# Moving two row sums from ScalarE to VectorE and four elementwise steps from VectorE to GpSimd in the last stage of a transformer layer

## The reference

```python
def quantize_e4m3(t, scale):
    return jnp.clip(t / scale, -FP8_MAX, FP8_MAX).astype(_FP8_DTYPE)
...
scores = jnp.einsum('bhqd,bhkd->bhqk', q, k) / np.sqrt(HD)
attn = jax.nn.softmax(scores.astype(jnp.float32), axis=-1)
out = jnp.einsum('bhqk,bhkd->bhqd', attn, v)
...
x_mat = quantize_e4m3(x2d, SCALE).astype(jnp.float16)
w_mat = quantize_e4m3(weight, SCALE).astype(jnp.float16)
out2d = (x_mat @ w_mat.T).astype(jnp.float32) * (SCALE * SCALE)
out2d = out2d + bias
...
x = _layernorm(x + _L0_attn_ref(...), axis=-1)
x = _layernorm(x + _L0_ffn_ref(x, L0_ffn_weight, L0_ffn_bias), axis=-1)
```

## Time and profile before

| | us |
|---|---|
| median of 2 timed runs | 1343.76 (1337.73 to 1349.79) |
| profiled execution | 1351.19 |
| its span on the slowest core (core 2) | 1349.6 |
| spans of the 8 cores | 1334.7 to 1349.6 |

### The profile page before, as it was taken

How to read it: one execution, slowest core, us unless ns; L and a number is a source line. 1 busy time by engine, 2 the same in 40 slices (tenths; PEclk the granted TensorE clock), 3 DMA queues, 4 the chain that set the end, 5 groups by cost and what they waited for, 6 DMA issues and landing times.

```text
span 1349.6 us, 11600 instructions; the slowest of 8 cores (1334.7 to 1349.6 us)
## 1 busy us (share of the span) xinstructions
PE 828.8 (61%) x3584; PEld 288.8 (21%) x3584; DVE 501.8 (37%) x942; ACT 724.7 (54%) x793; POOL 127.6 (9%) x66
## 2 busy tenths in 40 slices
PE   0588768595000587878878777877877723433334
PEld 0333323242000122222222222222222201111111
DVE  4267758621334112111211211121121165555566
ACT  0000000000221788888888888888888785555554
POOL 0046647500000000000000000000000000000000
PEclk9787767687555799999899999999999956666777
DMA  9732251203600000000000000000000000000001
GB/s 146 115 53 49 40 117 32 62 0 88 207 31 31 16 1 0 1 1 1 1 1 1 1 0 1 0 1 1 0 1 0 1 16 16 31 32 32 32 32 78
DMA packets 15131, 42.79 MB, mean 32 GB/s; under 512 B 2144, under 2 KB 2272, under 8 KB 15072
## 3 DMA queue, kind: packets, MB, share of 16 engines
q0 software_dynamic: 6624, 15.73, 6.7%
q1 hardware_dynamic: 8448, 26.33, 6.6%
HBM read 36.81 MB, written 8.39 MB: 33 GB/s over the span
## 4 chain that ended last, share of the span: by engine, by line
PE 31%; ACT 28%; DVE 14%; DMA 9%; issue 8%; POOL 7%; SPq 2%; ACTq 0%; DVEq 0%; POOLq 0%
ACT PT L397 18%; PE ps L412 14%; PE ps_sc L384 9%; PE ps L283 5%; DMA wfs<-wfT 3%; DMA srep_s<-srep 3%; POOL rs L248 2%; POOL rs L246 2%; POOL ro L249 2%; PE ps L219 1%; DVE zf L658 1%; SPq L261 1%; DMA wb<-wqT 1%; DVE zf L663 1%; DMA qT<-ro 1%
## 5 line engine op out<-in xcount | busy, mean ns | idle before, releaser
L397 ACT ACTIVATE PT<-ps_sc,k_s 128x1024 bf16<-128x1024 f32 x512 | 544.5, 1110 | 85.3 <-PE ps L412 47.4
L384 PE MATMUL ps_sc<-qT,kT 64*128 64x512 bf16 x1024 | 199.1, 388 | 228.3 <-ACT PT L397 215.6
L412 PE MATMUL ps<-PT,va 128*65 128x512 bf16 x1024 | 324.0, 399 | 24.5 <-ACT PT L397 24.2
L318 ACT ACT_TABLE_LOAD x1 | 1.3, 1283 | 336.2 <-DMA wfs<-wfT 336.2
L651 PE MATMUL ps<-wfq,yqT 128*128 128x512 bf16 x256 | 90.2, 531 | 141.0 <-ACT yqT L641 141.0
L219 PE MATMUL ps<-xT,wb 128*128 128x512 bf16 x512 | 147.2, 463 | 37.0 <-DVE qraw L230 30.2
L427 DVE COPY oa_sb<-ps 65x1024 f32<-65x1024 f32 x32 | 39.1, 1221 | 345.0 <-PE ps L412 345.0
L384 PEld LDWEIGHTS ps_sc<-qT,kT 64*128 64x128 bf16 x1024 | 58.5, 93 | 438.8 <-issue 436.6
L412 PEld LDWEIGHTS ps<-PT,va 128*65 128x65 bf16 x1024 | 72.6, 110 | 158.4 <-issue 158.4
L219 PEld LDWEIGHTS ps<-xT,wb 128*128 128x128 bf16 x512 | 57.9, 114 | 125.9 <-issue 125.9
L446 DVE RECIPROCAL rc_sb<-ps 128x1 f32<-128x1 f32 x256 | 20.1, 150 | 171.1 <-PE ps L434 171.0
(11 more groups left out here) (76 smaller groups left out, 581.1 us busy)
## 6 DMA issues: line engine op xcount, KB each, us to landing
xf<-x SPq DMA_DIRECT2D x1, 8192.0 KB, 33.2
out<-xf SPq DMA_DIRECT2D x16, 512.0 KB, 2.6
xb<-x POOLq DMA_DIRECT2D x1, 4096.0 KB, 33.4
qT<-ro SPq DMA_DIRECT2D x32, 128.0 KB, 2.4
kT<-ro SPq DMA_DIRECT2D x32, 128.0 KB, 2.4
wfs<-wfT POOLq DMA_DIRECT2D x8, 512.0 KB, 3.7
wb<-wqT POOLq DMA_DIRECT2D x1, 2048.0 KB, 17.9
wb<-wkT POOLq DMA_DIRECT2D x1, 2048.0 KB, 16.4
```

The source lines that it names most:

```text
L384: return e.matmul(ps_sc[:, slot, half * 512:(half + 1) * 512], kT[r0:r0 + 64, hp, kt * 128:(kt + 1) * 128], qT[r0:r0 + 64, hp, q0:q0 + 512 ...
L397: return e.activation(PT[:, slot, :], ps_sc[:, slot, :], AF.Exp, bias=consts[:, C_SHIFT:C_SHIFT + 1], scale=0.125)
L412: return e.matmul(ps1[0:65, base:base + 512], va[:, kt, h * 65: h * 65 + 65], PT[:, slot, half * 512:(half + 1) * 512], start=(kt == 0), s ...
```

## The change

`sum` and `sum2` become `reduce_sum` on DVE, and the ACT instructions that accumulated them go; `sq` and `sq2` stay on ACT and take over the waits. `qM`, `qE`, `qMt` and `z2` are the same instructions issued on POOL ("GC") instead of DVE. Everything else stands in the same order.

```diff
--- before.py
+++ after.py
@@ -547,16 +547,14 @@
         c0 = (st % 4) * 4
         c2_ = 16 + par * 4
         if stg == 0:
-            deps = [attn_done, t_wfq, rot_use["st1"].get(st % 4),
-                    rot_use["dump"][0]]
-            tk["sum"] = A("S", lambda e: e.activation(wfs[:], xf[:, st, :], AF.Copy,
-                                                      bias=0.0, scale=1.0,
-                                                      accum_out=stat[:, c0:c0 + 1]),
+            deps = [attn_done, t_wfq, rot_use["st1"].get(st % 4)]
+            tk["sum"] = A("V", lambda e: e.reduce_sum(stat[:, c0:c0 + 1], xf[:, st, :],
+                                                      axis=mybir.AxisListType.X),
                           waits=deps)
             tk["sq"] = A("S", lambda e: e.activation(wfs[:], xf[:, st, :], AF.Square,
                                                      bias=0.0, scale=1.0,
                                                      accum_out=stat[:, c0 + 1:c0 + 2]),
-                         waits=[tk["sum"]])
+                         waits=deps + [rot_use["dump"][0]])
             rot_use["dump"][0] = tk["sq"]
         elif stg == 1:
             tk["mean"] = A("V", lambda e: e.tensor_scalar_mul(stat[:, c0 + 2:c0 + 3],
@@ -595,13 +593,13 @@
                                                      scale=1.0), waits=[tk["qA"]])
         elif stg == 3:
             qs = qs_t if par == 0 else qs2
-            tk["qM"] = A("V", lambda e: e.tensor_scalar(qs[:, 0, :], qs[:, 1, :],
-                                                        consts[:, C_ILN2:C_ILN2 + 1],
-                                                        63.5, ALU.mult, ALU.add),
+            tk["qM"] = A("GC", lambda e: e.tensor_scalar(qs[:, 0, :], qs[:, 1, :],
+                                                         consts[:, C_ILN2:C_ILN2 + 1],
+                                                         63.5, ALU.mult, ALU.add),
                          waits=[tk["qL"], t_k])
-            tk["qE"] = A("V", lambda e: e.tensor_scalar(qs[:, 1, :], qs[:, 0, :],
-                                                        cder[:, 0:1], cder[:, 1:2],
-                                                        ALU.add, ALU.subtract),
+            tk["qE"] = A("GC", lambda e: e.tensor_scalar(qs[:, 1, :], qs[:, 0, :],
+                                                         cder[:, 0:1], cder[:, 1:2],
+                                                         ALU.add, ALU.subtract),
                          waits=[tk["qM"], t_C67])
             tk["qS"] = A("S", lambda e: e.activation(qs[:, 0, :], qs[:, 1, :], AF.Exp,
                                                      bias=0.0,
@@ -610,8 +608,8 @@
         elif stg == 4:
             qs = qs_t if par == 0 else qs2
             ys = st % 6
-            tk["qMt"] = A("V", lambda e: e.tensor_scalar(qs[:, 1, :], qs[:, 0, :], 1.0,
-                                                         cder[:, 0:1], ALU.max, ALU.mult),
+            tk["qMt"] = A("GC", lambda e: e.tensor_scalar(qs[:, 1, :], qs[:, 0, :], 1.0,
+                                                          cder[:, 0:1], ALU.max, ALU.mult),
                           waits=[tk["qS"]])
             tk["qP"] = A("V", lambda e: e.scalar_tensor_tensor(qs[:, 0, :], yf[:, ys, :],
                                                                512.0, qs[:, 1, :],
@@ -660,18 +658,19 @@
                 waits=[last, t_bf, rot_use["zf"].get(zs)])
             rot_use["ffn"][par] = tk["z1"]
             ys = st % 6
-            tk["z2"] = A("V", lambda e, zs=zs, ys=ys: e.tensor_add(
+            tk["z2"] = A("GC", lambda e, zs=zs, ys=ys: e.tensor_add(
                 zf[:, zs, :], zf[:, zs, :], yf[:, ys, :]), waits=[tk["z1"]])
             rot_use["yf"][ys] = tk["z2"]
         elif stg == 7:
             zs = st % 4
-            deps = [tk["z2"], rot_use["st2"].get(par), rot_use["dump"][0]]
-            tk["sum2"] = A("S", lambda e, zs=zs: e.activation(
-                wfs[:], zf[:, zs, :], AF.Copy, bias=0.0, scale=1.0,
-                accum_out=stat[:, c2_:c2_ + 1]), waits=deps)
+            deps = [tk["z2"], rot_use["st2"].get(par)]
+            tk["sum2"] = A("V", lambda e, zs=zs: e.reduce_sum(
+                stat[:, c2_:c2_ + 1], zf[:, zs, :], axis=mybir.AxisListType.X),
+                waits=deps)
             tk["sq2"] = A("S", lambda e, zs=zs: e.activation(
                 wfs[:], zf[:, zs, :], AF.Square, bias=0.0, scale=1.0,
-                accum_out=stat[:, c2_ + 1:c2_ + 2]), waits=[tk["sum2"]])
+                accum_out=stat[:, c2_ + 1:c2_ + 2]),
+                waits=deps + [rot_use["dump"][0]])
             rot_use["dump"][0] = tk["sq2"]
             tk["mean2"] = A("V", lambda e: e.tensor_scalar_mul(
                 stat[:, c2_ + 2:c2_ + 3], stat[:, c2_:c2_ + 1], 1.0 / D),
```

## The result

The changed kernel takes 1407.9 us (median of 11 runs, 1405.1 to 1418.2) beside 1340.3 us of the kernel before (median of 10, 1336.7 to 1353.9). The ratio is 1.051, 95% interval 1.048 to 1.055: 68 us slower. The forecast was 1334 us with a range of 1312 to 1378. The sign was wrong, and the time lies outside the range. Times here are medians of all runs of a kernel, while ratios and their intervals leave out runs in which some cores ran slower at a lower clock, so the two need not agree to the last digit.

The account below looks back on a forecast made before the run. A token passed between DVE and ACT was taken to bound the last stage, 17.21 us a round. Ten rounds saving 11.9 us, with +2 at the edges, gave -10: 1334 us against the timed 1343.8; range 1312 to 1378.

Parts of the forecast that it names:

- The ring: Last stage: DVE and ACT hand one token to and fro, so a round takes 8.36 + 8.85 = 17.21 us.
- The sums hidden on DVE: Full rounds: two reductions at 1.2 us stay hidden on DVE with 1 us to spare; ACT's half loses 2.48 us.
- z2 at 2.11: z2 on POOL, between z1 and qP, takes 2.11 us, read from a bf16 tensor_tensor row.
- The price a: Time of one tensor_scalar on POOL, occurring three times a round (qMt, qM, qE), taken as 1.2 us.
- upper bound: A tensor_scalar on POOL takes at most 2.11 us, the time of a tensor_tensor there.
- The sum's own formula: A full round after the change takes 12.42 + 3a, 16.02 us with a = 1.2, against 17.21 before.
- R1: Rival: POOL's tensor_scalar costs 2.11 us like its tensor_tensor; a round is 18.75, total +31, 1375 us; chance 0.24.
- The L606 no longer decides: y is late next: In a round, ACT's L606 after qE starts at 8.1, earlier by 0.3; y, starting at 9.78, decides instead.
- Turns: DVE's qP and qQ alternate with POOL's qM and qE, whole instructions at a time, each 0.14 shorter than alone.
- R2: Rival: DVE's qP and qQ run beside POOL's qM and qE without turns; -2.96 a round, 1314 us; chance 0.12.
- Edges: Outside the ten full rounds: filling -1, three shorter rounds even, the last two +1.4 and +1.2; together +2 us.
- About five more rounds: In their dependence on a, the edges count as about five more rounds: whole change -10 + 45 x (a - 1.2).

Follow-up runs that it names:

- the probe: Kernel before, with GpSimd and DVE instruction forms timed on scratch tiles beside the start of attention; 1495 us, of which only its rows count.
- the run with cheap pairs: Changed kernel with qE and qMt replaced by a mult and add of the same shape on GpSimd; 1337.8 us, ratio 0.994.

## Why the prediction was wrong, point by point

- **The ring** (17.21 = 8.36 + 8.85) was read rightly: the sums alone gave 14.72, qM off the ring 13.87, both as added up from the earlier trace rows.
- **The sums hidden on DVE** with 1 us to spare: right. A reduction takes 1.21 (taken: 1.2), and 1.54 us of DVE's wait is left in the run with the sums alone.
- **z2 at 2.11**: it took 2.34 in f32, where the row was bf16; +0.2 a round.
- **The price a of GpSimd's tensor_scalar is the step that failed.** I took one a = 1.2 for three instructions, between 0.75 and 2.11. For qM it holds (1.11 in the probe, alone). qMt took 3.71 and qE 3.78, beyond the "upper bound" of 2.11, and that bound was no bound: it compared the amount of data with another instruction's, and said nothing of what the engine does per element. Together 8.60 instead of 3.6, 5.0 us a round. The sum's own formula with the measured prices gives 12.42 + 0.23 + 8.60 = 21.25, beside 20.97 measured: the mis-sized term is enough for the whole loss and its sign. R1, "POOL is dear", had the direction and the place, and was mis-sized for the same reason: it priced a at 2.11.
- **"The L606 no longer decides: y is late next"** fell with it. With qE at 4.65 from start to start POOL's own chain ends after y, by 1.3 us, and is the ring. In the run with cheap pairs y and qS come level, and the sentence's sum (16.02) is met by 16.01. That agreement is in part luck: qZ (L622) started 8.36 after z1 and not 9.18, because qP had won its turn, and was then held for the 0.8 that the sum had not given it, so y stood at 9.79 beside 9.78.
- **Turns.** Right in substance, held. In detail qM lost its first turn to qP (2.15 and 1.24, not 1.2 and 2.2), qQ and qZ were held 0.64 and 0.8, and the slow forms hold DVE for only a part of their length, by 0.8 at their start. In the run with z2 alone the held instruction was qP. R2, no turns, is excluded. One row was read too simply: at 104.61 POOL was not idle; its L246 started at 104.65 and was the one held (2.63). So 0.69 is L241 when it goes first, and the reading (turns) stands.
- **Edges.** +2 was worked out for a = 1.2, and there they measured +5 in the run with cheap pairs: filling -2.4, three short rounds +0.5, and +5.7 in the last two instead of 2.6, +1 at the end. "About five more rounds" for a dearer a was too little too: outside the ten full rounds the changed kernel lost 30 us, 8 rounds' worth of 3.76. A short round has only one sum to shed, as the prediction says itself: the first of them went from 14.73 to 19.72, +5.0 where a full round lost 3.76. The sum had let them come out even.
- **The two rules named.** The Trainium skill, "GPSIMD Engine Reference", § Engine selection, has one-input work at roughly line rate; the trace agrees for qM's pair (1.11) and contradicts it for qE's (3.78), and the measurement decides. The Trainium skill, "SBUF — State Buffer", § Who interferes with whom, is borne out in whom it names: two tensor inputs are held, a reduction is not, and one small instruction shows both sides (0.95 against 0.21). In its "whole instruction" it is borne out for GpSimd's tensor_tensor and its fast forms, and not for the slow ones: L621 was held for 0.8 of L600's 3.78, L581 behind it not at all, and L694 for 0.5 near the end. There the measurement decides.

## What to carry to other kernels

Price every instruction that changes engine by its own operations, and by a probe of that form where the trace has none: on GpSimd the same shape with two column operands took 1.19 or 3.78 us by its pair of ALU operations. If two engines hand a token to and fro, moving work between engines gains only what leaves the ring: move what is hidden beside a wait (the sums, qM), not what the next instruction waits for (qMt) or is held by (z2). And beside GpSimd, look at DVE's instructions with two tensor inputs, the 128x1 ones included.

## What was not expected of the hardware

- GpSimd, 128x1024 f32: a tensor_scalar with mult and add 1.04 us, with one operation less 2.77, and with add and add 3.63. Writing add c0, subtract c1 as two passes of mult by 1 and add took 2 x 1.12 + 0.17 = 2.41 instead of 3.78.
- A 128x1 tensor_tensor on DVE took 1.05 us beside GpSimd's 1.12 us passes, and 0.16 without them.
- GpSimd's slow forms hold DVE for a part of their 3.7 us only: by 0.8 at their start (L621), not in the middle (L581), and a tensor_scalar again by 0.5 near their end (L694). Its tensor_tensor and its fast forms held DVE until they ended (by 1.96 on qP beside z2; four tensor_tensors in 7.33 us and not in 5.96).
